# A pair-interaction tower: first loads reordered, and a field's rows asked for when three of the four gathers in front have landed

## Chip, cores and metric

One core of one Trainium2 chip runs the kernel. The metric is device time in microseconds of one execution, lower is better. 1% of it is about 3.8 us.

## The reference

A batch of 512 samples has 40 categorical fields. Each field's id picks a row of 64 floats from that field's table. For every one of the 780 pairs of fields (i < j) the pair has its own 64x64 matrix W, and the result for a sample is one number:

```
e   = stack([tbl_f[ids[:, f]] for f in 0..39])        # 512 x 40 x 64
z_p = sum over d of (e[:, i_p, :] @ W[p]) * e[:, j_p, :]   # 512 x 780
h   = concat([z, dense_ctx], axis=1)                  # 512 x 796
h   = relu(h @ W_top1 + b_top1)                       # 796 -> 512
h   = relu(h @ W_top2 + b_top2)                       # 512 -> 256
y   = h @ W_top3                                      # 256 -> 1
```

All of it is float32.

## The kernel before, in words

The 40 fields are taken two at a time as 20 **items** (blocks) k = 0..19. Item k becomes one tile `xt[:, k, :]` of 128 partitions (2 fields x 64) by 512 samples. Each pair of items (i, k) is a **cell** with four field pairs.

**How an item is made.** The fields of items 0, 2 and 4 (`SMALL_BLOCKS`) have tables of 1000 rows. They are looked up by multiplication: DVE makes eight one-hot tiles for an item (line 388, `look_up`), and PE multiplies the table by them (line 300, 32 instructions for an item). At most `OHR` = 7 one-hots stand at once. DVE needs `row_sb` (a 4 KB table of row numbers) and `ids_bc` (the ids of the two fields on all partitions, 512 KB for each item); PE needs `small_sb` (512 KB for each item; for item 0 it comes in two loads of 256 KB). The other 17 items (`GATHERED` = 1, 3, 5, 6, 7, ...) are gathered by Pool (line 241): one indirect DMA brings 128 rows of 256 bytes, so a field takes `BT` = 4 of them and an item takes 8. The buffer `gath` has `GR` = 4 places. PE then transposes the rows by four instructions (line 287). Either way the item stands in the PSUM tile `xp`, and ACT copies it to `xt` (line 251) before `xp` is used again.

**Order on Pool.** The first gather waits for `ids_sb` (80 KB). In item g (counted among the gathered ones) the first field's four gathers are issued when all eight of item g - 1 have landed, and the second field's four when the first's four have landed. All add 16 to `gathered[g % GR]`. From the fifth gathered item on, Pool also waits until PE has used the buffer.

**Order on PE.** `form_item(k)` is placed before slot `item_slot(k)`: item 0, item 1 and item 2 before the first cell; then the cell of (0, 1) and a diagonal slot (lines 313 and 314, the pairs inside items 0 and 1); then item 3; then four cells, among them the two of k = 2; then a slot, item 4, and so on, each item two slots before its own first cell. A cell is four instructions of `fill` (line 324), DVE multiplies its 128x1024 result by `xt[:, k]` (line 405), and PE sums the products over partitions into `zp` by `sum_batch` (line 339, 16 instructions for four cells). A later item k takes part in k cells, so the PE work between two items grows with k. The tail (lines 355 to 372) is the three dense layers.

**Order on the load queues.** SP issues, without any wait: `ids_sb`, `row_sb`, two loads of `small_sb` for item 0, `ident_sb` (64 KB), `ids_bc` and `small_sb` for item 2, the first piece of pair matrices `w_ring` (8 cells, 512 KB), `sel_sb`, `ids_bc` and `small_sb` for item 4, `wd_sb` (320 KB, the diagonal slots' matrices), and seven more pieces of `w_ring`. Further pieces wait until the piece eight before has been used, and after piece 12 come the weights of the dense layers (`w1`, 1792 KB, and others). ACT issues only the `ids_bc` load of item 0, on its own queue.

Of the kernel before, what the change touches and what calls it, by code (L numbers as in the profile page):

```python
# [14 lines left out]
BT = B // P  # L15
# [49 lines left out]
GR = 4  # L65
# [18 lines left out]
def batch_slot(b):  # L84
    return CHUNK_SLOT[batch_end(b) - 1]
# [28 lines left out]
def program(nc, ids, ids_small, small, row_of, w_cell, w_diag, tables, w1, w2, w3, b1, b2, dense, ident, sel, out):  # L114
    with ExitStack() as ctx:
        def sb(name, shape, dt=F32):
            return ctx.enter_context(nc.sbuf_tensor(name, shape, dt))
# [4 lines left out]
        def sem(name):  # L122
            return ctx.enter_context(nc.semaphore(name))
# [4 lines left out]
        row_sb = sb("row_sb", [P, TC])  # L128
        w_ring = sb("w_ring", [P, RW, PIECE * P])
        wd_sb = sb("wd_sb", [P, NB // 2, D])  # L130
# [14 lines left out]
        ids_bc = late[:, 2 * NSM * TC * D:2 * NSM * (TC * D + B)].bitcast(I32).rearrange("p (f n) -> p f n", n=B)  # L145
# [12 lines left out]
        row_in = sem("row_in")  # L158
        small_in = [sem(f"small_in{s}") for s in range(NSM)]
        small_first_in = sem("small_first_in")  # L160
        ids_bc_in = [sem(f"ids_bc_in{s}") for s in range(NSM)]
        ident_in = sem("ident_in")
        sel_in = sem("sel_in")
        diag_in = sem("diag_in")
        w_in = [sem(f"w_in{r}") for r in range(RW)]
        tower_in = sem("tower_in")
        gathered = [sem(f"gathered{r}") for r in range(GR)]
        hot_ready = sem("hot_ready")
        hot_used = sem("hot_used")
        item_done = sem("item_done")  # L170
# [17 lines left out]
        @block.sync  # L188
        def _(sp):
            def load_small(s):  # L190
                sp.dma_start(ids_bc[:, 2 * s:2 * s + 2, :],
                             ids_small[:, 2 * s:2 * s + 2, :]).then_inc(ids_bc_in[s], 16)
                sp.dma_start(small_sb[:, 2 * s:2 * s + 2, :, :],
                             small[:, 2 * s:2 * s + 2, :, :]).then_inc(small_in[s], 16)

            def load_w(q):
                if q >= RW:
                    sp.wait_ge(u_filled, PIECE_LAST[q - RW] + 1)
                sp.dma_start(w_ring[:, q % RW, :], w_cell[q]).then_inc(w_in[q % RW], 16)

            sp.dma_start(ids_sb[:, :, :], ids).then_inc(ids_in, 16)
            sp.dma_start(row_sb[:, :], row_of).then_inc(row_in, 16)
            sp.dma_start(small_sb[:, 0:2, 0:TC // 2, :], small[:, 0:2, 0:TC // 2, :]).then_inc(small_first_in, 16)
            sp.dma_start(small_sb[:, 0:2, TC // 2:TC, :], small[:, 0:2, TC // 2:TC, :]).then_inc(small_in[0], 16)
            sp.dma_start(ident_sb[:, :], ident).then_inc(ident_in, 16)
            load_small(1)
            load_w(0)
            sp.dma_start(sel_sb[:, :], sel).then_inc(sel_in, 16)
            for s in range(2, NSM):
                load_small(s)  # L210
            sp.dma_start(wd_sb[:, :, :], w_diag).then_inc(diag_in, 16)
            for q in range(1, NP):
                load_w(q)
                if q == W1_AT:
                    sp.wait_ge(item_done, SMALL_BLOCKS[-1] + 1)
                    sp.dma_start(w1_sb, w1).then_inc(tower_in, 16)
                    sp.dma_start(w2_sb, w2).then_inc(tower_in, 16)
                    sp.dma_start(w3_sb[:, :], w3).then_inc(tower_in, 16)
                    sp.dma_start(b1_sb[:, :], b1).then_inc(tower_in, 16)
                    sp.dma_start(b2_sb[:, :], b2).then_inc(tower_in, 16)  # L220
                    sp.dma_start(z_sb[P - DENSE:P, NZ - 1, :], dense).then_inc(tower_in, 16)
            sp.wait_ge(y_ready, 1)
            sp.dma_start(out, y_sb).then_inc(stored, 16)
            sp.wait_ge(stored, 16)

        @block.gpsimd
        def _(pool):
            pool.wait_ge(ids_in, 16)
            for g, k in enumerate(GATHERED):
                if g:  # L230

                    pool.wait_ge(gathered[(g - 1) % GR], 16 * 2 * BT * ((g - 1) // GR + 1))
                if g >= GR:
                    pool.wait_ge(item_done, GATHERED[g - GR] + 1)  # L234
                for half in range(2):
                    f = 2 * k + half
                    if half:

                        pool.wait_ge(gathered[g % GR], 16 * BT * (2 * (g // GR) + 1))
                    for t in range(BT):  # L240
                        pool.indirect_dma_start(  # L241
                            gath[:, g % GR, t, half, :], None, tables[f],
                            bass.IndirectOffsetOnAxis(ap=ids_sb[:, t, f:f + 1], axis=0),
                        ).then_inc(gathered[g % GR], 16)

        @block.scalar
        def _(act):
            act.dma_start(ids_bc[:, 0:2, :], ids_small[:, 0:2, :]).then_inc(ids_bc_in[0], 16)
            for k in range(NB):
                act.wait_ge(item_done, k + 1)  # L250
                act.activation(xt[:, k, :], xp[:, :], ACT.Copy).then_inc(x_ready, 1)  # L251
                for t in range(NZ):

                    last = batch_slot(min(BANK_BATCHES * (t + 1), NBATCH) - 1) + LAG + 4
                    if k < NB - 1 and FIRST_SLOT[k] <= last < FIRST_SLOT[k + 1] and t < NZ - 1:
                        act.wait_ge(summed, BANK_BATCHES * (t + 1))
                        act.activation(z_sb[:, t, :], zp[:, :], ACT.Copy).then_inc(z_ready, 1)  # L257
            taken = sum(1 for t in range(NZ - 1)
                        if batch_slot(BANK_BATCHES * (t + 1) - 1) + LAG + 4 < FIRST_SLOT[NB - 1])
            for t in range(taken, NZ - 1):  # L260
                act.wait_ge(summed, BANK_BATCHES * (t + 1))
                act.activation(z_sb[:, t, :], zp[:, :], ACT.Copy).then_inc(z_ready, 1)  # L262
            act.wait_ge(summed, NBATCH)
            act.activation(z_sb[0:P - DENSE, NZ - 1, :], zp[0:P - DENSE, :], ACT.Copy).then_inc(z_ready, 1)
            act.wait_ge(tower_in, 16 * 6)
            for m in range(0, M1, 2):
                act.wait_ge(h1_mm, m + 1)
                act.activation(h1_sb[:, m, :], h1_ps[:, m, :], ACT.Relu,
                               bias=b1_sb[:, m:m + 1]).then_inc(h1_act, 1)
            act.wait_ge(h2_mm, 1)  # L270
            act.activation(h2_sb[:, 0, :], h2_ps[:, 0, :], ACT.Relu,
                           bias=b2_sb[:, 0:1]).then_inc(h2_act, 1)
            act.wait_ge(y_mm, 1)
            act.activation(y_sb, y_ps, ACT.Copy).then_inc(y_ready, 1)  # L274

        @block.tensor
        def _(pe):
            def form_item(k):
                if k:
                    pe.wait_ge(x_ready, k)  # L280
                if k in GATHERED:
                    g = GATHERED.index(k)
                    pe.wait_ge(ident_in, 16)
                    pe.wait_ge(gathered[g % GR], 16 * 2 * BT * (g // GR + 1))
                    for t in range(BT):
                        rows = gath[:, g % GR, t, :, :].rearrange("p a d -> p (a d)")
                        mm = pe.transpose(xp[:, t * P:(t + 1) * P], rows, ident_sb[:, :])  # L287
                    mm.then_inc(item_done, 1)
                    return
                s = SMALL_BLOCKS.index(k)  # L290
                if s == 0:
                    pe.wait_ge(small_first_in, 16)
                else:
                    pe.wait_ge(small_in[s], 16)
                for c in range(TC):
                    if s == 0 and c == TC // 2:
                        pe.wait_ge(small_in[0], 16)
                    pe.wait_ge(hot_ready, TC * s + c + 1)
                    for half in range(2):
                        mm = pe.matmul(xp[half * D:half * D + D, :], small_sb[:, 2 * s + half, c, :],  # L300
                                       one_hot[:, (TC * s + c) % OHR, half, :], start=c == 0, stop=c == TC - 1)
                    if c < TC - 1:
                        mm.then_inc(hot_used, 1)
                mm.then_inc(item_done, 1)
# [38 lines left out]
            for n in range(NS):  # L343
                for k in range(NB):
                    if item_slot(k) == n:
                        form_item(k)
                fill(n)
                for b in batches_after(n):
                    sum_batch(b)
# [169 lines left out]
```

## Time and profile before

| what | value |
|---|---|
| time, median of 3 runs | 379.32 us (377.79 to 379.42) |
| time of the profiled execution | 380.55 us |
| its span, first to last instruction | 378.4 us |
| mean granted TensorE clock | 0.977 |
| PE busy | 350.6 us (93%) |
| DVE busy | 252.8 us (67%) |
| POOL busy | 129.7 us (34%) |

The times in the profile are counted from the first instruction of the span. What lies outside the span is 380.55 - 378.4 = 2.15 us. A granted clock of 1.00 is 2.4 GHz and 0.50 is 1.2 GHz. An engine's busy share is a mean over stages that have different limits, so the stages have to be read one by one.

### The profile page before, as it was taken

Reading aid. Unit: us, or ns where it says so; the run is one execution under the profiler, and the core shown is the slowest. Engines: PE = TensorE matmul, PEld = TensorE weight load, DVE = VectorE, ACT = ScalarE, POOL = GpSimd, SP = SyncE. Lnnn points to the kernel's source line nnn. Section 1 sums busy time; section 2 is a strip of 40 time slices with the busy share of each in tenths; the row PEclk is TensorE's granted clock in tenths of the full one; section 3 lists DMA queues with packets and bytes.
Section 4 is the critical chain, followed back from the end, with each engine's and each line's share of the span. In section 5 each row is a group of like instructions: output and inputs, shape, how many; then the busy total and the mean of one; then the engine's idle time right before and its main releaser. Section 6 shows DMA issues by size and latency. Waiting matters only on the chain.

```text
span 378.4 us, 4408 instructions
## 1 busy us (share of the span) xinstructions
PE 350.6 (93%) x1820; PEld 120.1 (32%) x1820; DVE 252.8 (67%) x237; ACT 19.8 (5%) x32; POOL 129.7 (34%) x140
## 2 busy tenths in 40 slices
PE   2639899989996999999999999999999999999997
PEld 0212323223332333233333323333333333323442
DVE  3701958748774778877979778788888887890010
ACT  1000000000010000100000000000000000001011
POOL 3344665655563546456564565200000000000000
PEclk9968999989998999999999999999999999999999
DMA  7941112202217312222122221210000000000000
GB/s 267 408 190 21 19 21 75 79 18 78 77 38 304 80 25 67 75 73 78 30 69 75 69 78 21 69 57 1 2 0 0 2 0 2 0 0 2 0 0 0
DMA packets 10564, 23.37 MB, mean 62 GB/s; under 512 B 3489, under 2 KB 4257, under 8 KB 10418
## 3 DMA queue, kind: packets, MB, share of 16 engines
q1 hardware_dynamic: 6050, 18.12, 13.4%
q0 software_dynamic: 4352, 4.47, 5.8%
q10 hardware_dynamic: 144, 0.52, 0.5%
q8 instruction: 14, 0.23, 0.3%
q14 instruction: 4, 0.03, 0.0%
HBM read 23.09 MB, written 0.00 MB: 61 GB/s over the span
## 4 chain that ended last, share of the span: by engine, by line
PE 66%; POOL 13%; DMA 11%; issue 7%; DVE 1%; ACT 0%; POOLq 0%
PE u L324 35%; PE zp L339 19%; POOL gath L241 13%; DMA gath<-in_tbl,ids_sb 10%; PE u L355 6%; PE u L365 2%; PE xp L287 2%; PE u L313 2%; DMA ids_sb<-in_ids 1%; DVE prod L405 1%; PE xp L370 0%; PE xp L372 0%; ACT late L262 0%; ACT prod L274 0%; POOLq L234 0%
## 5 line engine op out<-in xcount | busy, mean ns | idle before, releaser
L405 DVE TENSOR_TENSOR prod<-u,xt 128x1024 f32<-128x1024 f32 x190 | 220.9, 1217 | 68.1 <-PE u L324 65.7
L324 PE MATMUL u<-xt,w_ring 64*128 64x512 f32 x760 | 184.6, 616 | 0.8 <-DVE prod L405 0.7
L241 POOL DMA_INDIRECT gath<-in_tbl,ids_sb x136 | 129.5, 952 | 110.3 <-DMA gath<-in_tbl,ids_sb 73.6
L324 PEld LDWEIGHTS u<-xt,w_ring 64*128 64x128 f32 x760 | 68.0, 187 | 105.9 <-DVE prod L405 52.4
L339 PE MATMUL zp<-prod,sel_sb 128*32 128x512 f32 x780 | 94.4, 599 | 0.7 <-ACT late L262 0.7
L339 PEld LDWEIGHTS zp<-prod,sel_sb 128*32 128x32 f32 x780 | 20.5, 109 | 69.0 <-issue 42.9
L300 PE MATMUL xp<-xt,late 128*64 128x512 f32 x96 | 25.4, 690 | 9.4 <-DMA late<-in_small 6.9
L388 DVE TENSOR_SCALAR xt<-late,row_sb 128x1024 f32<-128x1024 int32 x24 | 16.5, 748 | 18.3 <-PE xp L300 11.9
L287 PE MATMUL xp<-ident_sb,gath 128*128 128x128 f32 x68 | 12.0, 302 | 14.8 <-DMA gath<-in_tbl,ids_sb 14.8
L251 ACT ACTIVATE xt<-xp 128x512 f32<-128x512 f32 x20 | 12.0, 598 | 258.5 <-PE xp L287 207.8
L355 PE MATMUL u<-late 128*128 128x512 f32 x56 | 24.3, 594 | 0.0
L416 DVE TENSOR_SCALAR prod<-u,b_sb 128x512 f32<-128x512 f32 x2 | 1.5, 750 | 25.8 <-PE u L355 25.8
L287 PEld LDWEIGHTS xp<-ident_sb,gath 128*128 128x128 f32 x68 | 7.7, 149 | 28.2 <-issue 28.2
L300 PEld LDWEIGHTS xp<-xt,late 128*64 128x64 f32 x96 | 8.3, 160 | 25.1 <-issue 14.0
L355 PEld LDWEIGHTS u<-late 128*128 128x128 f32 x56 | 10.6, 190 | 13.8 <-issue 13.8
L313 PE MATMUL u<-xt,wd_sb 64*64 64x512 f32 x20 | 10.7, 614 | 0.0
L314 PE MATMUL u<-xt,wd_sb 64*64 64x512 f32 x20 | 10.7, 614 | 0.0
L397 DVE TENSOR_TENSOR prod<-u,xt 64x512 f32<-64x512 f32 x10 | 6.9, 695 | 3.8 <-PE u L314 2.0
L399 DVE TENSOR_TENSOR prod<-u,xt 64x512 f32<-64x512 f32 x10 | 6.8, 683 | 0.3
L365 PE MATMUL u<-prod,late 128*128 128x512 f32 x16 | 7.0, 592 | 0.0
L419 DVE TENSOR_SCALAR prod<-u,b_sb 128x512 f32<-128x512 f32 x1 | 0.8, 750 | 6.1 <-PE u L365 6.1
L257 ACT ACTIVATE late<-zp 128x512 f32<-128x512 f32 x5 | 3.0, 595 | 34.2 <-PE zp L339 34.2
(17 smaller groups left out, 14.6 us busy)
## 6 DMA issues: line engine op xcount, KB each, us to landing
w_ring<-in_w_cell SPq DMA_DIRECT2D x24, 512.0 KB, 3.3
gath<-in_tbl,ids_sb POOLq DMA_INDIRECT x136
late<-in_w_top SPq DMA_DIRECT2D x1, 1792.0 KB
late<-in_ids_small SPq DMA_DIRECT2D x2, 512.0 KB, 7.3
late<-in_small SPq DMA_DIRECT2D x2, 512.0 KB, 8.2
late<-in_ids_small ACTq DMA_DIRECT2D x1, 512.0 KB, 5.1
late<-in_small SPq DMA_DIRECT2D x2, 256.0 KB, 5.0
late<-in_w_top SPq DMA_DIRECT2D x1, 512.0 KB
```

The costliest lines, as they stand in the source:

```text
L241: pool.indirect_dma_start(gath[:, g % GR, t, half, :], None, tables[f], bass.IndirectOffsetOnAxis(ap=ids_sb[:, t, f:f + 1], axis=0),).then ...
L251: act.activation(xt[:, k, :], xp[:, :], ACT.Copy).then_inc(x_ready, 1)
L287: mm = pe.transpose(xp[:, t * P:(t + 1) * P], rows, ident_sb[:, :])
L300: mm = pe.matmul(xp[half * D:half * D + D, :], small_sb[:, 2 * s + half, c, :], one_hot[:, (TC * s + c) % OHR, half, :], start=c == 0, sto ...
L313: pe.matmul(u[D:P, n % UR, 0, :], wd_sb[0:D, i, :], xt[0:D, 2 * i, :], start=True, stop=True)
L314: pe.matmul(u[0:D, n % UR, 1, :], wd_sb[D:P, i, :], xt[D:P, 2 * i + 1, :], start=True, stop=True).then_inc(u_filled, 1)
L324: mm = pe.matmul(u[:, n % UR, a, :], w_ring[rows, q % RW, at * P:(at + 1) * P], xt[rows, i, :], start=True, stop=True)
L339: mm = pe.matmul(zp[32 * g:32 * g + 32, :], sel_sb[:, 30 - 2 * s:62 - 2 * s], prod[:, n % PR, a, :], start=s == 0, stop=last)
L355: mm = pe.matmul(h1_ps[:, m, :], w1_sb[:, t, m * P:(m + 1) * P], z_sb[:, t, :], start=t == 0, stop=t == NZ - 1)
L365: mm = pe.matmul(h2_ps[:, m, :], w2_sb[:, t, m * P:(m + 1) * P], h1_sb[:, t, :], start=t == 0, stop=t == M1 - 1)
L388: dve.tensor_scalar(one_hot[:, h % OHR, :, :], ids_bc[:, 2 * s:2 * s + 2, :], row_sb[:, c:c + 1], None, ALU.is_equal).then_inc(hot_ready, 1)
L405: dve.tensor_tensor(prod[:, n % PR, :, :], u[:, n % UR, :, :], x, ALU.mult).then_inc(prod_ready, 1)
```

## The change

There are four edits.

1. The `ids_bc` load of item 0 moves from ACT's queue to second place on SP's, and `row_sb` moves from second place on SP's queue to ACT's.
2. On SP's queue `wd_sb` moves ahead of the `ids_bc` and `small_sb` loads of item 4; and before these two SP waits until all eight gathers of the first gathered item have landed. All later loads stand behind that wait.
3. Each field's fourth gather adds to a semaphore of its own, `gathered_last`. Pool's waits go by `gathered` alone, which counts the other three: a field's gathers are issued when the first three of the field in front have landed. PE waits for both semaphores.
4. For the first gathered item (g = 0) the wait between its two fields is gone.

```diff
+        gathered_last = [sem(f"gathered_last{r}") for r in range(GR)]
...
             sp.dma_start(ids_sb[:, :, :], ids).then_inc(ids_in, 16)
-            sp.dma_start(row_sb[:, :], row_of).then_inc(row_in, 16)
+            sp.dma_start(ids_bc[:, 0:2, :], ids_small[:, 0:2, :]).then_inc(ids_bc_in[0], 16)
...
             sp.dma_start(sel_sb[:, :], sel).then_inc(sel_in, 16)
+            sp.dma_start(wd_sb[:, :, :], w_diag).then_inc(diag_in, 16)
+
+            sp.wait_ge(gathered[0], 16 * 2 * (BT - 1))
+            sp.wait_ge(gathered_last[0], 16 * 2)
             for s in range(2, NSM):
                 load_small(s)
-            sp.dma_start(wd_sb[:, :, :], w_diag).then_inc(diag_in, 16)
             for q in range(1, NP):
                 load_w(q)
...
             for g, k in enumerate(GATHERED):
                 if g:
-                    pool.wait_ge(gathered[(g - 1) % GR], 16 * 2 * BT * ((g - 1) // GR + 1))
+                    pool.wait_ge(gathered[(g - 1) % GR], 16 * 2 * (BT - 1) * ((g - 1) // GR + 1))
                 if g >= GR:
                     pool.wait_ge(item_done, GATHERED[g - GR] + 1)
                 for half in range(2):
                     f = 2 * k + half
-                    if half:
-                        pool.wait_ge(gathered[g % GR], 16 * BT * (2 * (g // GR) + 1))
+                    if g and half:
+                        pool.wait_ge(gathered[g % GR], 16 * (BT - 1) * (2 * (g // GR) + 1))
                     for t in range(BT):
                         pool.indirect_dma_start(
                             gath[:, g % GR, t, half, :], None, tables[f],
                             bass.IndirectOffsetOnAxis(ap=ids_sb[:, t, f:f + 1], axis=0),
-                        ).then_inc(gathered[g % GR], 16)
+                        ).then_inc((gathered if t < BT - 1 else gathered_last)[g % GR], 16)
...
-            act.dma_start(ids_bc[:, 0:2, :], ids_small[:, 0:2, :]).then_inc(ids_bc_in[0], 16)
+            act.dma_start(row_sb[:, :], row_of).then_inc(row_in, 16)
...
-                    pe.wait_ge(gathered[g % GR], 16 * 2 * BT * (g // GR + 1))
+                    pe.wait_ge(gathered[g % GR], 16 * 2 * (BT - 1) * (g // GR + 1))
+                    pe.wait_ge(gathered_last[g % GR], 16 * 2 * (g // GR + 1))
```

## Rows read from the trace of the kernel before

**Rows 1.** The page: its span and the chain's shares by engine.
```profile
span 378.4 us, 4408 instructions
...
PE 66%; POOL 13%; DMA 11%; issue 7%; DVE 1%; ACT 0%; POOLq 0%
```

**Rows 2.** Waits (us in total, times, longest) of PE 16:121, POOL, PE 121:343.
```profile
PE xp L287 <- DMA gath<-in_tbl,ids_sb: 14.8, 4, 8.9
...
POOL gath L241 <- DMA gath<-in_tbl,ids_sb: 73.6, 33, 5.3
...
PE u L324 <- DVE prod L405: 0.7, 2, 0.5
```

**Rows 3.** The chain in order of time: start us, us, what.
```profile
9.94 5.54 DMA gath<-in_tbl,ids_sb
...
19.61 5.06 DMA gath<-in_tbl,ids_sb
...
28.67 2.49 DMA gath<-in_tbl,ids_sb
...
113.99 5.98 DMA gath<-in_tbl,ids_sb
```

**Rows 4.** Timeline of POOL: start us, us, what [idle before <-releaser].
```profile
5.92 1.08 POOL L241 DMA_INDIRECT gath<-in_tbl,ids_sb  x1 [5.48 <-DMA ids_sb<-in_ids]
...
31.42 0.94 POOL L241 DMA_INDIRECT gath<-in_tbl,ids_sb  x1 [1.80 <-DMA gath<-in_tbl,ids_sb]
...
44.53 1.48 POOL L241 DMA_INDIRECT gath<-in_tbl,ids_sb  x1 [1.89 <-DMA gath<-in_tbl,ids_sb]
```

**Rows 5.** Timeline of PE, same columns.
```profile
6.94 8.96 PE L300 MATMUL xp<-xt,late 128*64 128x512 f32 x32 [6.94 <-DMA late<-in_small]
...
26.58 9.38 PE L300 MATMUL xp<-xt,late 128*64 128x512 f32 x32 [0.69 <-ACT xt L251]
...
37.96 0.66 PE L287 MATMUL xp<-ident_sb,gath 128*128 128x128 f32 x4
...
44.01 7.09 PE L300 MATMUL xp<-xt,late 128*64 128x512 f32 x32 [1.76 <-DVE xt L388]
...
77.56 0.63 PE L287 MATMUL xp<-ident_sb,gath 128*128 128x128 f32 x4 [2.44 <-DMA gath<-in_tbl,ids_sb]
78.12 4.54 PE L324 MATMUL u<-xt,w_ring 64*128 64x512 f32 x12
...
104.18 2.85 PE L324 MATMUL u<-xt,w_ring 64*128 64x512 f32 x12
...
120.11 1.09 PE L287 MATMUL xp<-ident_sb,gath 128*128 128x128 f32 x4 [2.96 <-DMA gath<-in_tbl,ids_sb]
121.12 2.08 PE L324 MATMUL u<-xt,w_ring 64*128 64x512 f32 x4
```

**Rows 6.** Windows: stretch, its length, busy of five engines, clock, DMA share, GB/s.
```profile
20.00:22.00 2.00, 0.00 (x0) 0.00 (x0) 0.00 (x0) 0.00 (x0) 0.55 (x1) 0.75 1.05 414
22.00:24.00 2.00, 0.00 (x0) 0.00 (x0) 0.00 (x0) 0.00 (x0) 0.00 (x0) 0.50 0.60 236
...
80.00:82.00 2.00, 2.00 (x8) 0.67 (x4) 1.52 (x2) 0.00 (x0) 1.52 (x2) 0.50 0.17 30
```

**Rows 7.** DMA: Pool's packets 28.7:29.9, 29.9:31.2, ACT's 0:4; two loads (last: us to landing).
```profile
q0 software_dynamic: 32, 0.03, 16.0%
...
q0 software_dynamic: 32, 0.03, 13.1%
...
q10 hardware_dynamic: 117, 0.46, 37.4%
...
w_ring<-in_w_cell SPq DMA_DIRECT2D x24, 512.0 KB, 3.3
...
ids_sb<-in_ids SPq DMA_DIRECT2D x1, 80.0 KB, 4.9
```

**Rows 8.** Timeline of DVE in the first 40 us.
```profile
6.04 10.65 DVE L388 TENSOR_SCALAR xt<-late,row_sb 128x1024 f32<-128x1024 int32 x15 [6.04 <-DMA row_sb<-in_row_of]
```

## The prediction

> **What bounds the kernel now.** I read the page first. PE is busy for 350.6 us of the 378.4 us span, yet the chain of work that ended last gives PE only 66%, and POOL and DMA together 24% [rows 1]. So part of the span is set by Pool's gathers. The chain in order of time says which part: it runs through gathers and their landings until 119.97 us, and after that only through PE [rows 3]. The waits say what it costs. Up to 121 us PE waited four times for gathers, 14.8 us in all, the longest 8.9 us; from 121 to 343 us it waited 0.7 us for DVE [rows 2]. The timeline of PE has two of the other three waits, 2.44 us before 77.56 and 2.96 us before 120.11 [rows 5], so the fourth is 14.8 - 8.9 - 2.44 - 2.96 = 0.5 us. The gather chain is therefore worth money up to 120 us only, and what the change gains or loses there moves the end one for one: the 258.3 us behind 120.11 are PE work.
>
> Pool itself is mostly waiting: 73.6 us in 33 waits for a landing [rows 2], one for each field. On a quiet DMA a field takes three steps of 1.25 us and the fourth gather's 2.49 us to landing [rows 3], with 0.26 us more until Pool goes on: 28.67 + 2.49 = 31.16 against 31.42 [rows 3, 4]. That is 6.5 us for a field, 13 us for an item. While the DMA engines are saturated (414 GB/s, until shortly after 22 us [rows 6]) the fourth gather lands 5.54 and 5.06 us after its issue began, and 5.98 us while the dense layers' weights are loaded [rows 3].
>
> **Field step in the steady part (edit 3).** Pool now waits for the third gather. Its landing has no row of its own. What there is: the 32 packets of the third gather of one field lie between 28.7 and 29.9 us and the 32 of the fourth between 29.9 and 31.2 us [rows 7], so each gather moves by itself, one step after the other. I take the third's latency to be the fourth's, 2.49 us. It then lands 1.25 us earlier, and Pool idles 1.80 - 1.25 = 0.55 us instead of 1.80 [rows 4]. The bounds are 0 (both land together) and 1.5 us, since the 0.30 us between two issues stays. A field then takes 5.25 us instead of 6.5. From item 3's landing to that of the item for which PE waits last lie six gathered items, 12 fields: 12 x 1.25 = 15 us less on Pool. PE's waits in that stretch are 2.44 + 0.5 + 2.96 = 5.9 us, so all three go, and the cover is about 9 us and more. What is late next is nothing of Pool's: PE's own work.
>
> **Clock given back.** After the 2.44 us wait the granted clock was 0.50 in 80:82 [rows 6], that is 1.2 GHz, and 12 instructions took 4.54 us where 12 like them take 2.85 at 2.4 GHz [rows 5]: 1.7 us. After the 2.96 us wait four transposes took 1.09 against 0.66 us, and four fills 2.08 us against a third of 2.85, 0.95 [rows 5]: 0.4 + 1.1 = 1.5 us. The 1.76 us wait before 44.01 was followed by 7.09 us of work against 9.38 us for the same 32 instructions after the long wait [rows 5], so short waits leave the clock alone. Without the waits these 3.2 us come back too.
>
> **The start (edits 1, 2, 4).** Four steps.
>
> First, `ids_sb`. Pool's first gather starts at 5.92 us, released by that load [rows 4], which landed 4.9 us after its issue [rows 7]. The first four microseconds hold 117 packets of ACT's queue, 0.46 MB, and these are `ids_bc` [rows 7], moved in turns with `ids_sb`. After the change ACT's queue has 4 KB. A load of 512 KB on a quiet DMA lands in 3.3 us [rows 7], so `ids_sb` lands 3.3 to 4.9 us after issue; I take 3.7, nearer the quiet row since the competitor is nearly gone. Pool starts at 4.7 us. `ids_bc` now stands between `ids_sb` and the table of item 0, and the bytes ahead of that table are the same: item 0 on PE starts near 6.9 us, give or take half a microsecond, and ends near 15.9 (6.94 + 8.96) [rows 5]. This cost lies beside the gathers.
>
> The Trainium skill ("DMA: Bandwidth & Descriptors", section "Queues, rings and completion order") says each DMA engine serves the queues it has work for in turn, a packet at a time. The row agrees as far as both queues show packets in the same stretch. With the fixed cost of about 2 us for a transfer that "SBUF — State Buffer" gives (section "The DMA setup-cost knee"), an estimate for `ids_sb` alone would be 2.2 us and the sum would come out 1.5 us lower than mine; no run here shows that.
>
> Second, the first gathered item. Its eight gathers now follow without a wait, at (9.94 - 5.92) / 3 = 1.34 us a step: the eighth begins at 4.7 + 7 x 1.34 = 14.1 us. SP's queue by then holds only some 3.1 MB instead of 7.6 (seven pieces of `w_ring` and item 4's two loads, 512 KB each, stand behind the wait), which at about 410 GB/s [rows 6] is through near 11 us. So the eighth lands with the quiet 2.49 us, at 16.6, where it landed at 19.61 + 5.06 = 24.67. PE has item 1 at 16.7 us. Its wait shrinks from 8.9 to about 0.8 us, and item 2 runs at 2.4 GHz: 7.09 instead of 9.38 us. With 1.3 us for the transposes and ACT's copy, item 2 ends near 25, and the cell and the diagonal behind it near 27 (before, they ran from 26.58 + 9.38 = 35.96 to 37.96 [rows 5], 2.0 us).
>
> Third, the wait of SP. SP passes it at 16.6 us; behind it are nine loads of 512 KB, 4.6 MB, from about 18 to 18 + 4.6 / 0.41 = 29 us. Needed first of these is item 4's pair, on DVE not before 37 us, and it is at the head. The next piece of `w_ring` is needed after item 4. Both are covered by more than 10 us. `wd_sb` and the first piece are ahead of the wait. But the saturated stretch is not gone; it has moved onto item 3's gathers.
>
> Fourth, item 3, which is where that collision is paid. Pool begins its first field when the seventh gather has landed, 12.8 + 2.49 + 0.26 = 15.5 us. The third gather begins at 18.0 and lands under load, plus 5.3 us (between 5.06 and 5.54): 23.3. The second field's gathers begin at 23.6, 24.9, 26.1 and 27.4. The fourth lands between 27.4 + 2.5 = 29.9 and 27.4 + 5.06 = 32.5 us. The nearest row is the gather of 19.61, which landed at 24.67, nearly 2 us after the DMA engines emptied: 29 + 2 = 31.0. PE, ready at 27, waits 4 us and starts item 3 at 31.0 instead of 37.96: 7.0 us less. After 4 us idle I expect the lower clock once more, as behind 2.44 and 2.96 us: 1.5 us given back, 0 to 1.7.
>
> **The sum**, against the profiled span: 378.4 - 7.0 - 5.9 - 3.2 + 1.5 = 363.8 us, 14.6 us less. The profiled execution took 380.55 us, 1.2 above the median of the runs; against the median it is 379.32 - 14.6 = 364.7 us. Reuse of the buffer adds nothing: Pool asks for a place that PE used four gathered items before, and is at most two to three ahead. The `w1` load will run beside gathers again, with over 10 us of cover.
>
> **The likeliest one's own range.** Low end: item 3 at 29.0 (the ids at 3.3 us, the quiet landing) and no lower clock, 18.1 us less: 361.2. High end: item 3 at 33.0, the lower clock, and 1 us for DVE, which multiplies for 1.2 us a cell where PE takes 1.4 and loses the pauses in which it caught up: 11.6 us less, 367.7.
>
> **Rivals.**
> *DVE's one-hots hold up the back-to-back gathers.* DVE runs 15 of them from 6.04 to 16.69 us [rows 8], right where the second field's gathers now stand. If these land only after that, the eighth is there at 16.69 + 2.49 = 19.2 us and SP's loads and item 3 shift by 2.6: item 3 at 33.6, 367.3 us. Against it: the first four gathers were issued and had landed by 9.94 + 5.54 = 15.5 us, under the same one-hots [rows 3]; for it: a gather's issue took 1.48 us once [rows 4], during item 4's one-hots. The Trainium skill's "SBUF — State Buffer" (section "Who interferes with whom") has such a rule, that a DVE instruction in a two-port mode locks GpSimd out while it writes descriptors; landings in the middle of the one-hots speak against a full lock.
>
> *The third lands no earlier than the fourth.* Then edit 3 does not do what it says. The start keeps its gain: item 3 lands near 32.6, Pool runs on from 32.7 where it ran on from 37.95, and keeps this 5.2 us lead at 6.5 us a field. PE's last wait ends at 120.1 - 5.2: 374.1 us. The packets speak against it [rows 7], since they come 1.25 us apart.
>
> *Slower: overlapping gathers cost Pool more.* If an issue takes e longer while another field's is under way, a field takes 5.25 + 4e. From 30.0 us, twelve fields, the last landed under the dense weights' load (5.98), end at 30 + 11 x 5.25 + 3.75 + 5.98 + 47e = 97.5 + 47e. It is later than 120.0 only from e = 0.48 us on. With the largest row, 1.48 - 0.94 = 0.54 us [rows 4], it is 122.9, the end 2.9 us later: 382.2. One issue of 136 shows that price, beside another engine's work.
>
> **Chances.** The forecast 0.76, the one-hots 0.09, the third with the fourth 0.07, dearer overlap 0.05, anything else 0.03. About 0.5% (1.9 us) is what a measurement of this kernel can tell from no change. Faster than that 0.92, within it 0.04, slower 0.04. The range is 361.2 to 370: it holds nearly all of the forecast's range and the one-hots' case, and leaves out the two others.
>
> **What would show it.** Right: Pool's first gather near 4.7 us, eight in a row, PE's item 1 near 16.7, item 3 near 31, about 0.5 us idle before each later field, no wait of PE for gathers after item 3, and a chain that names Pool only in the first 31 us. The `w_ring` loads on SP start near 17. Wrong: idle of about 1.8 us before each field (third with fourth), issues well over 0.94 us in the steady part (dearer overlap), item 1 near 19 us (one-hots), or PE waits for DVE that take the place of those for gathers. The weakest step is the landing of item 3 under the moved burst, 29 to 33 us.

## The result

The changed kernel took 401.25 us (median of 4 runs, 400.37 to 403.91) beside 378.56 us before (4 runs). The ratio is 1.0625, 95% interval 1.0546 to 1.0705: 6% slower, where 3.9% faster was forecast. In a later set of executions the same kernel took 362.96 us beside 377.24, ratio 0.9611 (0.9584 to 0.9637). The slower result came again in another set; the faster one was measured in one set, in all of its six runs. A *set* here means kernels run one after another on one chip, each beside the kernel before. The ratios leave out runs over 1.5% above the fastest of their kernel, so they aren't always the quotients of the medians.

The page of the profiled execution, 401.84 us, gives the span, the chain's shares and DMA issues:

```profile
span 399.7 us, 4426 instructions
...
PE 77%; another core or an unknown queue 6%; DVE 6%; issue 4%; DMA 3%; POOL 3%; ACT 0%; DVEq 0%
...
gath<-in_tbl,ids_sb POOLq DMA_INDIRECT x136
```

Beside [rows 1], Pool and DMA have gone from 24% of the chain to 6%, and something new stands in their place: 6% released by "another core or an unknown queue". There is one core. The words stand where a semaphore changed just as the wait ended, and no work that posts to it had ended shortly before. The chain in order of time has the places:

```profile
43.28 11.07 another core or an unknown queue
54.35 0.02 issue
...
62.77 12.73 another core or an unknown queue x2
75.50 0.02 issue
```

The timelines below call such a releaser "remote".

Pool's timeline, the rows where something other than the 0.30 us between two issues stands ahead of a gather:

```profile
2.95 1.08 POOL L244 DMA_INDIRECT gath<-in_tbl,ids_sb  x1 [2.50 <-DMA ids_sb<-in_ids]
...
14.41 1.42 POOL L244 DMA_INDIRECT gath<-in_tbl,ids_sb  x1 [1.23 <-DMA gath<-in_tbl,ids_sb]
...
23.76 0.94 POOL L244 DMA_INDIRECT gath<-in_tbl,ids_sb  x1 [3.74 <-DMA gath<-in_tbl,ids_sb]
...
35.47 0.94 POOL L244 DMA_INDIRECT gath<-in_tbl,ids_sb  x1 [0.45 <-DMA gath<-in_tbl,ids_sb]
...
76.38 0.94 POOL L244 DMA_INDIRECT gath<-in_tbl,ids_sb  x1 [5.33 <-remote]
```

This is what the change was to do: the first gather at 2.95 instead of 5.92 us, eight in a row, 0.45 us idle before a field instead of 1.80 [rows 4]. PE follows it for 45 us. Its timeline:

```profile
17.30 0.66 PE L291 MATMUL xp<-ident_sb,gath 128*128 128x128 f32 x4 [0.69 <-ACT xt L254]
18.64 7.09 PE L304 MATMUL xp<-xt,late 128*64 128x512 f32 x32 [0.69 <-ACT xt L254]
...
30.39 0.63 PE L291 MATMUL xp<-ident_sb,gath 128*128 128x128 f32 x4 [2.59 <-DMA gath<-in_tbl,ids_sb]
...
37.59 7.09 PE L304 MATMUL xp<-xt,late 128*64 128x512 f32 x32 [1.24 <-DVE xt L392]
...
55.66 2.08 PE L328 MATMUL u<-xt,w_ring 64*128 64x512 f32 x4 [6.00 <-issue]
...
63.54 2.08 PE L328 MATMUL u<-xt,w_ring 64*128 64x512 f32 x4 [4.76 <-DVE prod L401]
...
76.80 2.08 PE L328 MATMUL u<-xt,w_ring 64*128 64x512 f32 x4 [11.18 <-DVE prod L409]
```

Item 1 stands at 17.30, item 3 at 30.39 us (forecast: 16.7 and 31.0; before: 37.96 [rows 5]), and item 4 ends near 44.7. Then PE stops three times, 6.00 + 4.76 + 11.18 = 21.9 us, and each time no gather is what it waits for. It waits for DVE's products. So what does DVE wait for? Here are DVE, ACT and SP in their timelines:

```profile
54.38 1.23 DVE L409 TENSOR_TENSOR prod<-u,xt 128x1024 f32<-128x1024 f32 x1 [11.09 <-remote]
62.07 0.69 DVE L401 TENSOR_TENSOR prod<-u,xt 64x512 f32<-64x512 f32 x1 [6.47 <-issue]
...
75.52 4.63 DVE L409 TENSOR_TENSOR prod<-u,xt 128x1024 f32<-128x1024 f32 x4 [12.04 <-remote]
...
51.55 0.60 ACT L254 ACTIVATE xt<-xp 128x512 f32<-128x512 f32 x1 [19.90 <-remote]
75.64 0.60 ACT L254 ACTIVATE xt<-xp 128x512 f32<-128x512 f32 x1 [23.49 <-remote]
...
75.57 30.70 SPq L200 DMA_DIRECT2D w_ring<-in_w_cell  x3
```

ACT's copy at 51.55 waits for `item_done` of item 4, whose last matmul ended at 37.59 + 7.09 = 44.68 us: 6.9 us late. The copy at 75.64 is item 5's; PE had transposed it at 57.67 to 58.78: 17 us late. DVE's multiplication at 54.38 needs the fill that PE ran right behind item 4, and the one at 75.52 needs the fill that ran from 48.53 to 49.66. Near 75.5 us DVE, ACT and SP all go on within 0.12 us (75.52, 75.57, 75.64), and Pool at 76.38. What the four waits have in common is that PE posts the increment: `u_filled` for DVE and SP, `item_done` for ACT and Pool. What DVE posts reaches PE at once: DVE's 54.38 + 1.23 = 55.61, PE goes on at 55.66. So the work was done and its increments were held up. I call this *the hold-up*.

No view lists the increments, but the packed trace keeps the time at which each semaphore changed, and these times show it directly:

| PE's work in the result's trace | ended at | semaphore changed at |
|---|---|---|
| item 4's last matmul | 44.68 | 51.52 |
| fill of the cell behind it | 45.74 | 54.35 |
| the first two batches of `sum_batch` | 47.74, 48.60 | 75.35, 75.44 |
| fill of the next cell | 49.66 | 75.50 |
| fill of the cell at 55.66 | 57.74 | 75.56 |
| item 5's transposes | 58.78 | 75.62 |

The longest delay is 27.6 us, and the increments arrive in the order in which PE posted them. (The diagonal slot's between them has no record; PE had filled it by 46.8, and DVE went on with it at 62.07.) In the same trace no recorded increment of DVE or ACT inside the span is more than 0.01 us late.

### The profile page after: what moved, and what is told of

Its sections match the earlier page's. It is cut to its first block, busy times and chain, and to the rows that moved or that the text cites. A ratio compares the mean times of both kernels' runs of the same rounds, so it can differ in the third digit from the quotient of the medians.

```text
span 399.7 us, 4426 instructions
## 1 busy us (share of the span) xinstructions
PE 354.8 (89%) x1820; PEld 119.8 (30%) x1820; DVE 253.4 (63%) x237; ACT 19.9 (5%) x32; POOL 130.2 (33%) x140
## 4 chain that ended last, share of the span: by engine, by line
PE 77%; another core or an unknown queue 6%; DVE 6%; issue 4%; DMA 3%; POOL 3%; ACT 0%; DVEq 0%
PE u L328 42%; PE zp L343 23%; PE u L359 6%; DVE prod L409 4%; DMA gath<-in_tbl,ids_sb 3%; POOL gath L244 3%; PE xp L291 2%; PE u L317 2%; PE u L369 2%; DVE xt L392 1%; DMA ids_sb<-in_ids 0%; PE xp L374 0%; PE xp L376 0%; DVE prod L401 0%
## 5 line engine op out<-in xcount | busy, mean ns | idle before, releaser
L328 PE MATMUL u<-xt,w_ring 64*128 64x512 f32 x760 | 188.6, 624 | 27.5 <-DVE prod L409 15.3
L343 PE MATMUL zp<-prod,sel_sb 128*32 128x512 f32 x780 | 97.3, 615 | 0.7 <-ACT late L265 0.7
L304 PE MATMUL xp<-xt,late 128*64 128x512 f32 x96 | 22.9, 632 | 9.8 <-DVE xt L392 9.1
L420 DVE TENSOR_SCALAR prod<-u,b_sb 128x512 f32<-128x512 f32 x2 | 1.5, 751 | 25.8 <-PE u L359 25.8
L317 PEld LDWEIGHTS u<-xt,wd_sb 64*64 64x64 f32 x20 | 1.9, 131 | 9.2 <-DVE prod L409 6.2
```

The source lines that it names most:

```text
L317: pe.matmul(u[D:P, n % UR, 0, :], wd_sb[0:D, i, :], xt[0:D, 2 * i, :], start=True, stop=True)
L328: mm = pe.matmul(u[:, n % UR, a, :], w_ring[rows, q % RW, at * P:(at + 1) * P], xt[rows, i, :], start=True, stop=True)
L343: mm = pe.matmul(zp[32 * g:32 * g + 32, :], sel_sb[:, 30 - 2 * s:62 - 2 * s], prod[:, n % PR, a, :], start=s == 0, stop=last)
```

## The experiments

Six sets in all. The sets differ in whether the hold-up occurs, and that turned out to be the main finding, so each run is given with its set. The times are medians of all runs of a kernel, in us.

| set | kernel | time | before in the set | ratio (95%) | hold-up |
|---|---|---|---|---|---|
| 1 | the change | 401.25 | 378.56 | 1.0625 (1.0546 to 1.0705) | yes |
| 2 | e1 start only | 372.2 | 379.01 | 0.983 (0.9785 to 0.9874) | no |
| 2 | e2 edit 3 only | 368.63 | 379.01 | 0.9732 (0.9675 to 0.9788) | no |
| 2 | e3 split only | 387.91 | 379.01 | 1.0229 (1.0176 to 1.0281) | no |
| 2 | e4 Pool busy | 378.0 | 379.01 | 0.9994 (0.9965 to 1.0023) | no |
| 3 | e5 the change | 362.96 | 377.24 | 0.9611 (0.9584 to 0.9637) | no |
| 3 | e6 no SP wait | 364.17 | 377.24 | 0.9637 (0.9603 to 0.9672) | no |
| 3 | e7 first item waits | 368.0 | 377.24 | 0.9737 (0.9703 to 0.9772) | no |
| 3 | e8 old queues | 366.71 | 377.24 | 0.9714 (0.9681 to 0.9747) | no |
| 4 | e9 the change | 407.24 | 379.19 | 1.0621 (1.0551 to 1.0691) | yes |
| 4 | e10 matrices later | 408.92 | 379.19 | 1.0694 (1.0618 to 1.0771) | yes |
| 4 | e11 two landed | 405.86 | 379.19 | 1.0727 (1.0652 to 1.0803) | yes |
| 4 | e12 pause each item | 385.71 | 379.19 | 1.0185 (1.0131 to 1.0239) | yes |
| 5 | e13 start only | 373.69 | 377.53 | 0.9879 (0.9826 to 0.9933) | no |
| 5 | e14 edit 3 only | 368.88 | 377.53 | 0.9775 (0.9721 to 0.9829) | no |
| 5 | e15 even spacing | 369.07 | 377.53 | 0.9773 (0.97 to 0.9845) | no |
| 6 | e16 matrices later | 359.18 | 378.31 | 0.9508 (0.9451 to 0.9564) | no |
| 6 | e17 start only | 372.82 | 378.31 | 0.9858 (0.9797 to 0.9918) | no |
| 6 | e18 even spacing | 370.11 | 378.31 | 0.9791 (0.9714 to 0.9868) | no |

### Set 2: each part alone

**e1, the start without edit 3.**

```diff
-            sp.wait_ge(gathered[0], 16 * 2 * (BT - 1))
-            sp.wait_ge(gathered_last[0], 16 * 2)
+            sp.wait_ge(gathered[0], 16 * 2 * BT)
...
-                    pool.wait_ge(gathered[(g - 1) % GR], 16 * 2 * (BT - 1) * ((g - 1) // GR + 1))
+                    pool.wait_ge(gathered[(g - 1) % GR], 16 * 2 * BT * ((g - 1) // GR + 1))
```

(The wait between fields likewise, and every gather adds to `gathered`.)

> The changed kernel without edit 3: first loads reordered, SP's wait, no wait between the two fields of the first gathered item, but everywhere else all four gathers of a field must have landed. Theory A (gathers that follow each other without a pause of Pool, one always in flight, hold up the semaphore increments that PE posts): Pool pauses after each field, so nothing is held up. Item 3 on PE near 31.5 us, Pool about 6 us ahead of before from there on, so 371 to 374 us. Rival B (the moved loads and SP's wait are the fault): the 12 us idle stretches of PE between 50 and 77 us are there as in the changed kernel, 395 us or more.

372.2 us. The start as such costs nothing; it brings 6.8 us. PE waited 8.6 us for gathers in four waits, one of 2.6 us at item 3 and the three from before almost unchanged.

**e2, edit 3 on the kernel before.** Its diff is part 3 of the change.

> The kernel before with edit 3 alone: own semaphore for the fourth gather, Pool goes on when three of the four in front have landed; loads and first item as before. Theory A: PE idles in long stretches some 10 to 20 us after Pool's unbroken run begins, DVE, ACT and SP are released together at the end of a stretch, 390 to 405 us. Rival B: the fault lies in the start, which is as before here, so PE's waits of 5.9 us and 3.2 us of clock are saved: 369 to 372 us.

368.63 us, where theory A wanted 390 or more. The waits of PE in this kernel:

```profile
PE xp L289 <- DMA gath<-in_tbl,ids_sb: 7.8, 1, 7.8
```

One wait for gathers is left of the four in [rows 2], the one at the start. So an unbroken run of gathers doesn't by itself hold anything up. One of the four runs, which the ratio leaves out, took 1233.21 us. There is no trace of it.

**e3, the fourth gather's semaphore split off, Pool waiting for both.**

```diff
-                    pool.wait_ge(gathered[(g - 1) % GR], 16 * 2 * BT * ((g - 1) // GR + 1))
+                    pool.wait_ge(gathered[(g - 1) % GR], 16 * 2 * (BT - 1) * ((g - 1) // GR + 1))
+                    pool.wait_ge(gathered_last[(g - 1) % GR], 16 * 2 * ((g - 1) // GR + 1))
```

(The wait between fields and PE's wait likewise, and the fourth gather adds to `gathered_last`.)

> The kernel before with the fourth gather of each field on a semaphore of its own, but Pool still waits for both semaphores, so its timing is unchanged. Theory A: within 1 us of before. Rival C (four more semaphores, other semaphore numbers, or two waits where one was are what costs): slower by several us, up to the 22 us of the changed kernel.

387.91 us, 8.9 us slower: theory A's expectation missed, and rival C's held, through the last of its three causes and not through the hold-up. Pool's timeline, a field's first gather in the steady part:

```profile
53.69 0.94 POOL L244 DMA_INDIRECT gath<-in_tbl,ids_sb  x1 [2.29 <-DMA gath<-in_tbl,ids_sb]
```

Idle 2.29 us where the kernel before has 1.80 [rows 4]. A wait for two semaphores in place of one costs Pool about 0.5 us each time, on the chain that set the end: PE's last wait for gathers ends at 129.06 us, 8.95 us behind the 120.11 of before [rows 5]. The change itself has one wait there until Pool comes to reuse buffers.

**e4, Pool busy while the fourth gather lands.**

```diff
+                    if f_done:
+                        pool.wait_ge(idled, f_done)
+                    pool.memset(idle_sb[:, :], 0.0).then_inc(idled, 1)
+                    f_done += 1
```

> The kernel before, and Pool writes zeros to a spare tile (128x1280 float32, an estimated 1 to 2 us) after each field's fourth gather, while it lands. The landing is waited for as before. Theory A (gathers in flight without a pause are what counts): within 2 us of before, more only where the memset outlasts the landing. Rival D (a Pool that is busy without a pause, whatever it does, holds up PE's increments): long idle stretches of PE, 390 us or more.

378.0 us, no difference. The memset took 1184 ns and was done before the landing; Pool then rested 0.5 to 0.6 us before most fields. In this set so busy a Pool holds nothing up.

### Set 3: the change again, and three of its parts undone

**e5, the changed kernel, unaltered.**

> The changed kernel once more, unaltered, beside the kernel before on the same chip. Theory A2 (start and edit 3 together hold up the increments that PE posts, in every execution): 398 to 404 us and the same idle stretches of PE between 50 and 77 us. Rival E (the hold-up strikes some executions of any kernel whose gathers follow without a pause, as the 1233 us run of edit 3 alone suggests, and is no fixed part of the schedule): other executions run without it, at 361 to 366 us, which is what start and edit 3 are worth together (7 us and 11 us less than before, less what they share).

362.96 us, six runs from 362.18 to 364.00. Rival E held. PE's waits for gathers in it:

```profile
PE xp L291 <- DMA gath<-in_tbl,ids_sb: 3.6, 1, 3.6
```

Pool's start, and PE at items 1 and 3, in its timeline:

```profile
3.05 1.08 POOL L244 DMA_INDIRECT gath<-in_tbl,ids_sb  x1 [2.60 <-DMA ids_sb<-in_ids]
...
16.76 0.66 PE L291 MATMUL xp<-ident_sb,gath 128*128 128x128 f32 x4 [0.69 <-ACT xt L254]
...
30.83 0.94 PE L291 MATMUL xp<-ident_sb,gath 128*128 128x128 f32 x4 [3.57 <-DMA gath<-in_tbl,ids_sb]
```

Up to item 3 the two executions of the same kernel hardly differ (30.39 and 30.83 us). The windows of both show where they part. First the result's trace, then e5's, 45 to 80 us (busy of PE, PE weight loads, DVE, ACT, POOL; granted clock; DMA share; GB/s):

```profile
45.00:80.00 35.00, 13.06 (x52) 3.54 (x52) 7.08 (x7) 1.19 (x2) 22.13 (x24) 0.65 0.14 37
```

```profile
45.00:80.00 35.00, 35.00 (x204) 11.54 (x202) 26.97 (x25) 2.39 (x4) 23.92 (x26) 1.00 0.26 70
```

Pool did nearly the same (24 and 26 instructions). PE did 52 instead of 204. The 399.7 - 361.8 = 37.9 us between the spans are accounted for: PE's waits behind 45 us add up to 21.9, and 6.9 after 80 us, which e5 has none of; PE's busy time is 354.8 against 345.0 us, 9.8 more, mostly since the clock fell (0.65 in that stretch); and item 3's wait was 1.0 us shorter. 21.9 + 6.9 + 9.8 - 1.0 = 37.6.

**e6, SP's wait left out.** The two `sp.wait_ge` lines are gone.

> The changed kernel without SP's wait for the first gathered item: item 4's loads and seven pieces of matrices are issued at once, as before the change. Theory A2 (it is the gathers' unbroken run that counts): idle stretches stay, 390 us or more. Rival F (the late burst of loads behind SP's wait is what it takes): no idle stretches, 362 to 369 us, since item 1 lands later under load.

364.17 us, 1.2 more than with it. The wait helps little: item 1 stands at 18.00 instead of 16.76 us, item 3 at 31.17 instead of 30.83.

**e7, the wait inside the first gathered item put back.**

```diff
-                    if g and half:
+                    if half:
```

> The changed kernel with the wait put back between the two fields of the first gathered item, by its first three gathers. Theory A2: idle stretches stay, 390 us or more. Rival G (eight gathers in a row at the start, all in flight together, are what it takes): no idle stretches, 363 to 368 us.

368.0 us: leaving that wait out is worth 5.0 us.

**e8, the two loads back on their old queues.**

```diff
-            sp.dma_start(ids_bc[:, 0:2, :], ids_small[:, 0:2, :]).then_inc(ids_bc_in[0], 16)
+            sp.dma_start(row_sb[:, :], row_of).then_inc(row_in, 16)
...
-            act.dma_start(row_sb[:, :], row_of).then_inc(row_in, 16)
+            act.dma_start(ids_bc[:, 0:2, :], ids_small[:, 0:2, :]).then_inc(ids_bc_in[0], 16)
```

> The changed kernel with the row numbers' load back on SP's queue and the ids_bc load of item 0 back on ACT's. Theory A2: idle stretches stay, 390 us or more. Rival H (the exchanged queues are what it takes): no idle stretches, and the ids land at 5.7 us as before instead of 2.7, so 363 to 368 us.

366.71 us: the exchange is worth 3.8 us. The chain of e8 and then that of e5 has the ids' landing:

```profile
0.74 4.06 DMA ids_sb<-in_ids
```

```profile
0.74 2.03 DMA ids_sb<-in_ids
```

As no hold-up occurred in set 3 at all, e6 to e8 don't tell which part it takes. They only price the parts.

### Set 4: the hold-up again, and how it goes with pauses

**e9, the changed kernel a third time.**

> The changed kernel unaltered, a third time, in another job. Theory E (the hold-up is a condition of one set of executions, not of the schedule): 361 to 365 us again. Rival (the second set, at 362.96 us, was the exception): near 401 us.

407.24 us, seven runs from 401.89 to 411.48: theory E's number missed and the rival's, near 401, was the nearer one, so the hold-up is no accident of a single set. It strikes at the same place. DVE's timeline and SP's queue:

```profile
53.86 1.23 DVE L409 TENSOR_TENSOR prod<-u,xt 128x1024 f32<-128x1024 f32 x1 [11.06 <-remote]
60.24 0.69 DVE L401 TENSOR_TENSOR prod<-u,xt 64x512 f32<-64x512 f32 x1 [5.16 <-remote]
...
76.48 4.63 DVE L409 TENSOR_TENSOR prod<-u,xt 128x1024 f32<-128x1024 f32 x4 [14.83 <-remote]
...
76.54 35.72 SPq L200 DMA_DIRECT2D w_ring<-in_w_cell  x3
```

54.38, 62.07 and 75.52 in set 1, 53.86, 60.24 and 76.48 here. Pool's last gather before it waits for PE ends at 71.05 us in set 1; the release of all comes 4.5 us behind that. It is the same in e9 (the gather of 71.02 ends at 71.96, DVE goes on at 76.48) and in e10 (81.93 and 86.51): what has piled up is released together when Pool has issued no gather for 4.5 us.

**e10, the seven pieces of matrices later.**

```diff
                 load_small(s)
+            sp.wait_ge(gathered[1], 16 * 2 * (BT - 1))
+            sp.wait_ge(gathered_last[1], 16 * 2)
             for q in range(1, NP):
```

> The changed kernel, and SP's seven pieces of matrices wait until the second gathered item's rows have landed too; only item 4's two loads follow the first. Theory I (what limits item 3 is the landing of its gathers under the moved burst of loads): item 3's gathers lands near quiet speed, PE starts item 3 near 27.5 us instead of 30.8 and keeps its full clock, 358 to 360 us. Rival J (Pool's own rate or item 4's loads set it): item 3 stays near 30 us, 362 to 364 us.

408.92 us, with the hold-up. PE waited for no gather at item 3 any more, so the part that theory I speaks of held; its time had to be measured again (e16).

**e11, Pool goes on after two of four.** `BT - 2` for `BT - 1` in the waits and in the choice of the semaphore; 4 for 2 in the waits for `gathered_last`.

> The changed kernel, and Pool goes on when two of a field's four gathers have landed, so that it issues at 1.25 us a gather with no pause but 0.3 us. PE has no wait for gathers after item 3 any more, so by the prediction's mechanism 361 to 364 us, as the changed kernel. Theory A (an unbroken run of gathers holds up PE's increments): the hold-up shows in at least some executions, 380 us or more.

405.86 us, the hold-up in all four runs. Compared with e9 the last half microsecond of Pool's pauses made no difference beyond the spread of the runs.

**e12, a full wait between items.**

```diff
                     pool.wait_ge(gathered[(g - 1) % GR], 16 * 2 * (BT - 1) * ((g - 1) // GR + 1))
+                    pool.wait_ge(gathered_last[(g - 1) % GR], 16 * 2 * ((g - 1) // GR + 1))
```

> The changed kernel, and between two items Pool waits for all eight gathers again, so it pauses once for each item and only within an item goes on after three. Six items cost about 1.3 + 0.4 us more each than in the changed kernel, and the slack was over 9 us. So PE should wait nowhere behind item 3: 362 to 366 us. It tells what a pause each item would cost. If the clear gain needed every field's step, 368 us or more.

385.71 us. PE had no wait for gathers behind item 3, so by the forecast's mechanism 362 to 366 us. Pool paused some 2.3 us once an item, and PE still stopped:

```profile
DVE prod L410 <- remote: 11.2, 3, 5.3
```

In this set, then, the hold-up cost some 40 to 48 us without pauses (401.89 to 411.48 in e9, against 362.96 in set 3), some 20 with one pause an item, and nothing visible with one pause a field (before: 379.19 us, in sets without it 377.24 to 379.01). The longest delay of an increment, counted from the latest finished work that posts to the same semaphore and so at least this long, goes the same way: 28.2 us in e9, 27.9 in e10, 25.8 in e11, 3.8 in e12.

### Sets 5 and 6: what could not be told apart, and a better version

**e13 and e17, the start alone; e14, edit 3 alone.** The kernels are e1 and e2.

> The start alone (edits 1, 2 and 4), once more. If this job is one in which the hold-up occurs: theory A (gathers without a quiet moment between fields bring it about) says 371 to 373 us as in the first job, since Pool pauses after each field. Rival K (anything that speeds Pool's chain up brings it about) says 385 us or more. In a job without the hold-up both say 371 to 373 us.

> Edit 3 alone, once more. In a job with the hold-up, theory A says 390 to 410 us with idle stretches of PE and releases of DVE, ACT and SP together at their end. Rival L (the hold-up needs the start as well) says 368 us. In a job without it both say 367 to 369 us.

> The start alone. In a job with the hold-up, theory A (gathers without a quiet moment between fields) says 371 to 374 us, rival K (a faster gather chain of any kind) 385 us or more. In a job without it 371 to 374 us by both.

373.69, 372.82 and 368.88 us, as the first time within 1.5 us. Neither set had the hold-up, so these runs repeat the prices and tell nothing of what brings it about.

**e15 and e18, even spacing.**

```diff
+                        if g:
+                            if made:
+                                pool.wait_ge(idled, made)
+                            pool.memset(idle_sb[:, :], 0.0).then_inc(idled, 1)
+                            made += 1
```

> The changed kernel, and Pool writes zeros to 128x320 floats (0.35 us) after each gather from the second gathered item on. Gathers then follow every 1.6 us, 6.4 us a field, the rate of before, but the next is issued before the one in front has landed, so there is no quiet moment. In a job with the hold-up: theory A (no quiet moment) says 385 us or more. Rival M (too many gathers per time) says 370 to 375 us, as the start alone. Without the hold-up: 370 to 375 us.

> The changed kernel with Pool's short memset after each gather: about 6 us a field, never a moment without a gather in flight. In a job with the hold-up, theory A says 385 us or more, rival M (too many gathers per time) 368 to 375 us. In a job without it 367 to 371 us by both.

369.07 (0.9 us under its range) and 370.11 us, again without the hold-up in either set. Whether it is the missing quiet moment (theory A) or the number of gathers per time (rival M) stays open.

**e16, e10's kernel again.**

> The changed kernel, and SP's seven pieces of matrices wait for the second gathered item too. In a job without the hold-up: theory I (the landing of item 3's gathers under the moved burst is what limits the start) says 358 to 360 us; rival J says 362 to 364 us. In a job with the hold-up: 404 to 412 us, as in the third job.

359.18 us, ratio 0.9508 (0.9451 to 0.9564): the fastest version, 3.8 us below e5. Theory I held. PE starts item 3 at 27.24 us, its timeline has no wait for a gather left, and item 4 starts 5 us earlier than in e5 (38.23 us):

```profile
33.26 7.09 PE L306 MATMUL xp<-xt,late 128*64 128x512 f32 x32 [1.77 <-DVE xt L394]
```

Set 6 ran on the same chip as set 4. The same kernel, on the same chip, took 408.92 us there and 359.18 us here. So the chip is not what decides, nor the kernel alone.

**A sign of it in the profile.** The landing time at the end of the gathers' row in the DMA issues is missing in set 1 (before and after) and in all four kernels of set 4. It is there in all fourteen profiles of the sets without the hold-up. The rows of e9 and of e16:

```profile
gath<-in_tbl,ids_sb POOLq DMA_INDIRECT x136
```

```profile
gath<-in_tbl,ids_sb POOLq DMA_INDIRECT x136, 2.5
```

In the sets with the hold-up, then, records of events are lost: the six packed traces hold 1101 to 1705 records of landings, the fourteen others 2820 to 2846.

The same traces tell where PE's increments are late, counted in the same way within the span. In the fourteen none is recorded over 0.06 us late. In the changed kernel's trace of set 1, 60 are over 0.1 us late, and in the trace of the kernel before from that set 24 are, the latest by 1.1 us. So the kernel before meets the same condition; its increments come late too, but too little for its time to show it. In all six traces the last late increment comes before Pool's last gather ends or within 2 us of it.

The Trainium skill ("NOTIFIC — the notification-queue block", section "Overflow: three behaviours, one of which stalls the engine") says that the block through which engines write such records can, when its queue is full, discard a record or stall the engine that produces it. Lost records and held-up increments in the same executions would fit that. No run here shows it: no execution was taken without its records.

## Why the prediction was wrong

**The step that failed.** The sum ended with "all three [waits] go", and "what is late next is nothing of Pool's: PE's own work". It took for granted that PE's increments reach the others promptly, whatever Pool does. In sets 1 and 4 they came up to 27.6 and 28.2 us late while Pool gathered with pauses of 0.45 us: 37.9 us came on top of a sum that was right in set 3 (361.8 us of span, forecast 363.8). That case had no number of its own; it was in the 0.03 for anything else. One of the prediction's signs of being wrong did come, PE waits for DVE in place of those for gathers, but no mechanism stood behind it. The slower rival was the wrong mechanism. It wanted issues well above 0.94 us in the steady part, and they are 0.94, at most 1.02.

**The start.** `ids_sb` landed after 1.94 us, not 3.7. My bounds, 3.3 and 4.9 us, were both too high: the quiet row that I took was a 512 KB load, and I didn't scale it to 80 KB. From the fixed cost of about 2 us that the Trainium skill has ("SBUF — State Buffer", section "The DMA setup-cost knee") the prediction had an estimate of 2.2 us, and the measured 1.94 us is within 0.3 us of it. It moved the end little, since `ids_bc` became later by about a microsecond (item 0 from 7.51 us in e5, not 6.9) and item 1 came from PE and not from the gathers: 16.76 us, forecast 16.7.

**The moved burst.** Item 3 at 30.39 and 30.83 us, forecast 31.0, range 29 to 33. e10 and e16 show that the loads behind SP's wait are what it waited for. That it came out so close is partly luck: Pool began item 3's first field at 14.41 and 14.11 us, not 15.5, but its third gather took 5.68 and 5.61 us to land, more than the 5.06 to 5.54 that I had, and ate most of the lead.

**The field step.** Forecast 0.55 us idle, measured 0.45; PE's later waits all gone in e2 and e5. Right. e2 alone saved 10.4 us, where the waits and the clock behind them had 5.9 + 3.2 = 9.1.

**Clock given back.** The mean granted clock was 0.995 in e5 and 0.957 in the result. The lower clock behind item 3's wait came as forecast: in the result's trace the next 16 fill instructions took 5.40 us, where e16's, without that wait, took 3.70: 1.7 us, forecast 1.5. The row in the result's timeline of PE:

```profile
30.95 5.40 PE L328 MATMUL u<-xt,w_ring 64*128 64x512 f32 x16
```

**Buffer reuse** was said to add nothing. Pool did wait for PE in e5, 11.8 us in two waits, as it had run four items ahead. It cost nothing, being slack; in the hold-up it is the wait in which the stretch ends.

**The one-hots.** Ruled out: the eighth gather landed under them. Pool went on at 14.41 us, when the seventh had landed, and SP at 14.61, when all eight had, while the one-hots ran until 17.39 (6.96 + 10.43 us). SP's row:

```profile
14.61 0.33 SPq L192 DMA_DIRECT2D late<-in_ids_small  x1
```

**What stays open.** What makes a set one with the hold-up; whether the start or edit 3 alone suffers from it; whether quiet moments or the rate decide; and what held up the run of 1233 us. That PE's increments are late, and only while Pool gathers, stands in the traces. Why they are late doesn't; a cause in how the records are written is argued only.

## What to carry to other kernels

A change that removes pauses from one engine's DMA chain can be worth what the waits say and still be lost to a condition outside the kernel: time it in more than one set, and keep a version whose gain does not need it. The start alone gained 1.2 to 1.7% in three sets of three, none of them with the hold-up, so it isn't shown to be such a version; the change and the kernel of e16 gain 3.9 and 4.9% or lose 6 and 7%. When a wait names "another core" on a single core, or landings are missing from the page, list which engine posts what every late instruction waits for. And load what is needed first, first: 0.5 MB on another queue doubled the landing of 80 KB, and 3.7 MB of matrices placed one item later gained 3.8 us.

## What the hardware showed unexpectedly

Increments posted by PE arrived up to 27.6 us late in the result's trace while those of DVE released PE within 0.05 us, and DVE, ACT and SP were then released within 0.12 us, 4.5 us after Pool's last gather. The condition was there in two sets of six, and there in the kernel before too, by up to 1.1 us. On Pool a second semaphore in a wait cost about 0.5 us. A load of 80 KB landed in 1.94 us beside 4 KB on the other queue, and in 4.06 us beside 512 KB. Eight gathers in a row without a wait cost Pool little: their issue took 0.94 to 1.08 us in the result's trace, and the seventh landed 3.32 us after it began.
